# A new order of work in the chunks of a Mamba block, with a list of its own for the first chunk and loads of C waited for by groups

## The reference

```python
xi, z = split(x @ W_in.T)                        # 512 channels each
u = silu(causal_conv4(xi) + conv_b)
dbl = u @ W_xproj.T                              # 16 for dt, 16 for B, 16 for C
dt = softplus(dbl[..., :16] @ W_dt.T + b_dt);  A = -exp(A_log)
h = h * exp(dt * A) + (dt * u) * B;   y = sum_s h * C     # over 1024 tokens, 16 states
y = (y + u * D_skip) * silu(z)
x = layernorm(x + y @ W_out.T)
x = layernorm(x + (silu(x @ Wg.T) * (x @ Wu.T)) @ Wd.T)    # weights int / 127
```

## Time and profile before

| what | us |
|---|---|
| profiled execution | 1891.66 |
| its span | 1889.7 |
| first scan starts at | 34.3 |
| first chunk | 120.8 |
| steady chunks | 112.8 and 111.9 in turn |
| last chunk | 104.9 |
| from the last scan's end to the end of the span | 56.1 |
| busy: PE, DVE, ACT, POOL | 1763.2, 1708.9, 1656.7, 1498.0 |

### The profile page before, as it was taken

The page is one execution under the profiler, slowest core; times in us unless marked ns, Lnnn a source line. Parts: engine busy times, 40 slices in busy tenths (PEclk is TensorE's granted clock), DMA queues, the critical chain, the costliest instruction groups (busy, mean ns, idle before and its releaser), DMA issues.

```text
span 1889.7 us, 40293 instructions
## 1 busy us (share of the span) xinstructions
PE 1763.2 (93%) x15674; PEld 1218.9 (65%) x15674; DVE 1708.9 (90%) x1946; ACT 1656.7 (88%) x2892; POOL 1498.0 (79%) x847
## 2 busy tenths in 40 slices
...
GB/s 200 1 82 34 4 112 14 97 28 3 123 4 112 14 39 87 3 112 15 112 14 2 123 3 113 15 87 37 4 123 4 113 14 24 102 20 84 24 1 23
DMA packets 171341, 100.55 MB, mean 53 GB/s; under 512 B 139392, under 2 KB 157568, under 8 KB 162960
## 3 DMA queue, kind: packets, MB, share of 16 engines
...
## 4 chain that ended last, share of the span: by engine, by line
PE 48%; ACT 17%; DVE 17%; issue 11%; POOL 6%; DMA 0%; ACTq 0%; DVEq 0%; POOLq 0%
PE ring L1096 19%; PE tp L1075 14%; DVE h L846 8%; PE yb L1089 7%; ACT decay L641 6%; DVE acc L867 5%; ACT hT L648 5%; PE ring L1184 4%; POOL drive L512 3%; ACT acc L657 2%; ACT xi L659 1%; POOL diag_c L521 1%; ACT yt L669 1%; PE decay L1293 1%; ACT dt L695 1%
## 5 line engine op out<-in xcount | busy, mean ns | idle before, releaser
L512 POOL TENSOR_TENSOR drive<-dtu,b_all 128x1024 f32<-128x1024 f32 x512 | 1223.9, 2422 | 91.6 <-DVE h L846 78.8
L641 ACT ACTIVATE decay<-dt,a_neg 128x512 f32<-128x512 f32 x1024 | 707.8, 712 | 81.7 <-DVE h L846 80.6
L648 ACT ACTIVATE hT<-tp 128x512 f32<-128x512 f32 x1024 | 594.4, 611 | 81.9 <-PE tp L1075 80.8
L1075 PE MATMUL tp<-ident,h 128*128 128x128 f32 x4096 | 584.7, 280 | 80.5 <-ACT hT L648 71.0
L846 DVE TENSOR_TENSOR_SCAN h<-decay,h,drive 128x512 f32<-128x512 f32 x512 | 624.6, 1269 | 37.6 <-ACT decay L641 37.6
L846 DVE TENSOR_TENSOR_SCAN h<-decay,drive 128x512 f32<-128x512 f32 x512 | 597.2, 1211 | 61.4 <-ACT decay L641 44.1
L1075 PEld LDWEIGHTS tp<-ident,h 128*128 128x128 f32 x4096 | 465.5, 142 | 288.2 <-issue 140.3
L1089 PE MATMUL yb<-hT,diag_c 128*32 128x128 f32 x8192 | 275.5, 277 | 4.3 <-POOL diag_c L521 2.5
L1089 PEld LDWEIGHTS yb<-hT,diag_c 128*32 128x32 f32 x8192 | 210.7, 110 | 89.0 <-issue 53.2
L1096 PE MATMUL ring<-xt,w_in 128*128 128x512 f32 x512 | 241.9, 606 | 21.7 <-DVE yg L857 16.8
L867 DVE SCALAR_TENSOR_TENSOR acc<-xi,cw,acc 128x512 f32<-128x512 f32 x192 | 169.7, 898 | 14.8 <-ACT xi L659 10.8
(11 more groups left out here) (127 smaller groups left out, 1598.3 us busy)
## 6 DMA issues: line engine op xcount, KB each, us to landing
...
c_col<-bc_scratch SPq DMA_DIRECT2D x256, 2.0 KB, 2.4
...
```

Of the source, the lines that this page charges most:

```text
L512: tt(drive[:, j % 4, :, :], src, b_all[:, n:n + 2, :], ALU.mult).then_inc(g_dr, 1)
L641: act(decay[decay_slot(k.parity, i)][:, :], dt[:, cb, :], ACT.Exp, scale=a_neg[:, cb, n:n + 1]).then_inc(a_da, 1)
L648: act(hT[:, (64 * k.index + g) % HTS, :], tp[g % 2][:, :], ACT.Copy).then_inc(a_ev, 1)
L1075: last = nc.tensor.transpose(tp[g % 2][:, b * P:(b + 1) * P], h[:, h_slot(k.parity, q), t0:t0 + TS, :].rearrange("p t s -> p (t s)"), iden ...
```

## The change

The four steady tables are permuted. The first chunk gets tables of its own (`PE_FIRST`, `ACT_FIRST`, `DVE_FIRST`, `POOL_FIRST`), chosen by `table_of`. The tables of the last chunk and the lists of the end are reordered; `end_out 0 1` moves from the end list into the last chunk, `sz 3` and POOL's `gate 2` from the last chunk into the end lists. The loads of c_col count on four semaphores, one for each group of four states, and a diagonal waits for its group alone; in the first chunk each group's load of B goes directly before its four column loads.

```diff
 PE_SIDE = {
-    (0, 1): [("xi", 0), ("xi", 1), ("sum", 14)], (0, 3): [("xi", 2)], (1, 0): [("sum", 15), ("xi", 3), ("z", 0)],
-    (4, 3): [("out", 0)], (5, 0): [("out", 1)], (5, 2): [("sum", 3), ("xproj", 0)],
-    (6, 0): [("dt", 0), ("turn", 0)], (7, 0): [("x1T", 0), ("sum", 5)],
-    (14, 1): [("down", 0)], (14, 3): [("down", 1)],
+    (0, 1): [("xi", 0), ("xi", 1)], (0, 3): [("z", 0), ("sum", 14)], (3, 3): [("xi", 2), ("xi", 3)],
+    (4, 1): [("out", 0)], (4, 2): [("sum", 2), ("out", 1)], (4, 3): [("xproj", 0)],
+    (5, 2): [("sum", 3), ("dt", 0)], (5, 3): [("x1T", 0)], (6, 0): [("dt", 1), ("turn", 0)],
+    (14, 2): [("down", 0)], (15, 0): [("down", 1)],
...
 ACT_SIDE = {
-    (0, 0): [("log", 1)], (0, 1): [("hT", 60)], (0, 2): [("hT", 61), ("xi", 0)],
-    (0, 3): [("hT", 62), ("hT", 63)], (1, 0): [("xi", 1), ("xi", 2)], (1, 1): [("y", 3)], (1, 2): [("xi", 3)],
-    (5, 1): [("hT", 14), ("sz", 0), ("hT", 15), ("u", 0), ("u", 1), ("sz", 1), ("u", 2), ("sz", 2), ("hT", 16), ("sz", 3), ("u", 3)],
+    (0, 0): [("log", 1), ("hT", 60)], (0, 2): [("xi", 0), ("hT", 61), ("hT", 62), ("xi", 1), ("hT", 63)],
+    (3, 3): [("norm", 1), ("z", 3), ("hT", 10), ("hT", 11)], (4, 0): [("xi", 2), ("xi", 3)],
+    (4, 2): [("hT", 12), ("u", 0), ("sz", 0), ("sz", 1), ("u", 1), ("u", 2), ("sz", 2), ("u", 3), ("hT", 13)],
+    (5, 0): [("hT", 14), ("hT", 15), ("xproj", 0), ("hT", 16), ("hT", 17)],
+    (5, 1): [("norm", 0), ("hT", 18), ("bias", 0), ("y", 0), ("x1T", 0), ("hT", 19)], (5, 2): [("bias", 1)],
+    (8, 3): [("sz", 3)],
...
 DVE_SIDE = {
-    (0, 3): [("max", 1)], (2, 2): [("conv", 0, 0), ("conv", 0, 1)],
-    (5, 0): [("conv", 1, 0), ... , ("conv", 3, 0), ("r1", 0), ("conv", 3, 1)], (5, 2): [("r1", 1)],
-    (6, 1): [("skip", 0)], (13, 3): [("clamp", 0)], (15, 0): [("max", 0)],
+    (0, 3): [("conv", 0, 0)],
+    (4, 1): [("max", 1), ("conv", 0, 1), ("conv", 1, 0), ... , ("conv", 3, 0), ("conv", 3, 1)],
+    (4, 2): [("r1", 0)], (4, 3): [("r1", 1)], (5, 3): [("skip", 0)],
+    (13, 3): [("hid", 5), ("skip", 1)], (14, 0): [("clamp", 0), ("skip", 2)], (14, 3): [("max", 0)],
...
 POOL_SIDE = {
-    (5, 1): [("gate", 3), ("heads", 0), ("diag", 3)], (6, 1): [("std", 0)], (7, 0): [("gate", 0), ("dtu", 1)],
+    (4, 0): [("diag", 2), ("gate", 3)], (4, 1): [("heads", 0), ("diag", 3)], (5, 1): [("std", 0)],
+    (6, 1): [("dtu", 1)], (7, 1): [("gate", 0)],
...
+PE_FIRST = {
+    (0, 3): [("xi", 0), ("z", 0), ("xi", 1), ("z", 1), ("xi", 2), ("xi", 3), ("z", 2)], (1, 3): [("z", 3)],
...
+ACT_FIRST = {
+    (0, -1): [("xi", 0), ("z", 0), ("log", 1), ("z", 1), ("sz", 0), ("xi", 1), ("sz", 1), ("xi", 2), ("u", 0), ("z", 2)],
+    (0, 0): [("u", 1)], (1, 0): [("xi", 3), ("hT", 0)],
+    (7, 3): [("sz", 2), ("u", 2), ("hT", 28), ("sz", 3), ("u", 3)],
...
+DVE_FIRST = {
+    (0, -1): [("clamp", 1), ("conv", 0, 0), ("conv", 0, 1), ("conv", 1, 0), ("max", 1), ("conv", 1, 1), ("conv", 2, 0), ("conv", 2, 1)],
+    (7, 3): [("conv", 3, 0), ("conv", 3, 1), ("skip", 0)], (13, 2): [("skip", 1), ("clamp", 0)],
+    (14, 0): [("skip", 2)], (14, 1): [("max", 0)],
+POOL_FIRST = {
+    (0, -1): [("dtu", 1)], (2, 1): [("first_diag", 0)], (3, 0): [("first_diag", 1), ("first_diag", 2)],
+    (5, 0): [("first_diag", 3)], (8, 1): [("heads", 0)], (15, 0): [("gate", 0)],
+    (15, 1): [("gate", 1), ("dtu", 0), ("gate", 2), ("diag", 0)],
 PE_LAST = {
-    (14, 1): [("down", 0)], (14, 2): [("down", 1)], (15, 2): [("end_out", 0, 0)],
+    (12, 3): [("down", 0)], (13, 2): [("down", 1)], (14, 2): [("end_out", 0, 0)], (15, 1): [("end_out", 0, 1)],
 ACT_LAST = {
-    (5, 2): [("norm", 1), ("sz", 0), ("hT", 17), ("sz", 1), ("sz", 2), ("z", 3), ("hT", 18), ("sz", 3)],
+    (2, 2): [("sz", 0)], (12, 1): [("sz", 1), ("sz", 2)],
 ACT_END = [
-    ("hT", 57), ("hT", 58), ("hT", 59), ("end_hT", 60), ...
+    ("hT", 57), ("hT", 58), ("hT", 59), ("sz", 3), ("end_hT", 60), ...
 POOL_END = [
-    ("end_std", 1),
+    ("gate", 2), ("end_std", 1),

+def table_of(kind, steady, first, last):
+    return first if kind == "first" else last if kind == "last" else steady

-            def spread_bc(k, b_first=False):
+            def spread_bc(k, with_b=False):
                 wait(eng, a_dbl, k.count(2, 2))
                 eng.dma_start(bc_dram, dbl[R:R + 2 * N, :]).then_inc(st_bc, 16)
                 wait(eng, st_bc, k.count(16, 16))
-                if b_first:
-                    for g in range(4):
+                for g in range(4):
+                    if with_b:
                         load_b(g)
-                for n in range(N):
-                    g, s = n // 4, n % 4
-                    eng.dma_start(c_col[s:P - 3 + s:4, g, :], ...).then_inc(l_c, 16)
+                    for s in range(4):
+                        eng.dma_start(c_col[s:P - 3 + s:4, g, :], ...).then_inc(l_c[g], 16)
             def diagonals(k, g):
-                if g == 0:
-                    wait(eng, l_c, k.count(16 * N, 16 * N))
+                wait(eng, l_c[g], k.count(64, 64))
```

More of the change, by code:

```diff
@@ L62 @@
-    (15, 3): [("sum", 13)],
+    (0, 1): [("xi", 0), ("xi", 1)], (0, 3): [("z", 0), ("sum", 14)], (1, 0): [("sum", 15)], (1, 2): [("z", 1)],
+    (2, 0): [("z", 2), ("sum", 0)], (2, 1): [("turn", 3)], (3, 1): [("z", 3)], (3, 2): [("sum", 1)],
+    (3, 3): [("xi", 2), ("xi", 3)], (4, 1): [("out", 0)], (4, 2): [("sum", 2), ("out", 1)],
+    (4, 3): [("xproj", 0)], (5, 2): [("sum", 3), ("dt", 0)], (5, 3): [("x1T", 0)],
+    (6, 0): [("dt", 1), ("turn", 0)], (6, 1): [("sum", 4), ("x1T", 1), ("dt", 2), ("gate", 0)],
@@ L63 @@
+    (15, 0): [("down", 1)], (15, 3): [("sum", 13)],
 }
 ACT_SIDE = {
[18 rows of a table removed]
[18 rows of a table added]
 }
 DVE_SIDE = {
-    (0, -1): [("clamp", 1)], (0, 3): [("max", 1)], (2, 2): [("conv", 0, 0), ("conv", 0, 1)],
-    (3, 1): [("skip", 3)],
-    (5, 0): [("conv", 1, 0), ("conv", 1, 1), ("conv", 2, 0), ("conv", 2, 1), ("conv", 3, 0), ("r1", 0), ("conv", 3, 1)],
-    (5, 2): [("r1", 1)], (6, 1): [("skip", 0)], (7, 3): [("gs", 0)], (8, 1): [("hid", 0), ("gs", 1)],
-    (9, 0): [("hid", 1)], (9, 3): [("gs", 2)], (10, 0): [("hid", 2)], (10, 2): [("skip", 1)],
@@ L106 @@
-    (10, 3): [("gate", 3)], (11, 1): [("up", 3), ("gate", 4)], (11, 2): [("sum", 9)], (12, 0): [("gate", 5)],
-    (12, 2): [("sum", 10)], (12, 3): [("up", 4)], (13, 1): [("sum", 11)], (13, 2): [("up", 5)],
-    (14, 0): [("turn", 2)], (14, 1): [("down", 0)], (14, 2): [("down", 1)], (15, 0): [("sum", 12), ("sum", 13)],
-    (15, 2): [("end_out", 0, 0)],
+    (0, -1): [("z", 0)], (0, 0): [("sum", 14)], (1, 0): [("z", 1), ("sum", 15)], (2, 0): [("turn", 3)],
+    (2, 1): [("sum", 0)], (2, 2): [("out", 0)], (2, 3): [("out", 1)], (3, 1): [("z", 2)],
```

116 lines of the change are left out of this document (61 added, 55 removed), and 79 rows, old and new, of tables (ACT_FIRST, ACT_LAST, ACT_SIDE, DVE_LAST).

## The result

The kernel after takes 1844.06 us, the median of four runs (1842.64 to 1845.36), against 1891.05 us for the kernel before on the same chip: ratio 0.9757, 95% interval 0.9746 to 0.9769. The profiled execution took 1845.17 us, its span is 1843.2. Forecast was 1872 with a range of 1833 to 1901: the sign and the range held, the size did not. 47 us went, not 19.

What follows compares the result with a forecast made beforehand. No engine alone was taken to set the time but the order in which they meet, DVE being the steadiest pacer. Steady chunks -9, first -6, last -3, end -2 sum to -20 from 1891.66: 1872 us, range 1833 to 1901.

Steps and rivals of the forecast that it cites:

- The steady sum: Steady chunk: DVE loses 3.4 + 3.1 + 0.1 + 0.6 = 7.2 us against 7.8, 14 x -0.6 = -9 us.
- its list by place: DVE's losses per steady chunk before: 4.2 us in the opening, 3.0 behind the burst, 0.6 at chunk end: 7.8.
- Opening: Quads 0 to 2 of a steady chunk: DVE 3.4 us behind its bare work, against 4.2; bounds 2.0 and 5.8.
- The lone step: First convolution step in the steady opening: waits for xi 0 and, beside POOL's drives, up to one drive of 2.4 us.
- Burst and skip 0: Behind the steady convolution burst: skip 0 waits 2.6 us for its ring bank, with hand-overs 3.1, against 3.0.
- POOL idle at `heads` hides the burst: Steady chunk: `max` and eleven convolution steps, some 9.4 us, run while POOL waits at `heads`; its late drive 10 is covered.
- Lone silu: Slot (8,3), steady chunks: `sz 3` alone between decays adds two table loads, 2.6 us of ACT; DVE loses 0.1, bounds 0 and 2.6.
- Chunk end: Steady chunk's end: the 0.6 us loss for downs goes, the clamp beside POOL's last drives costs 0.6; bounds 0 and 4.5.
- First chunk, last chunk, end: Outside the steady chunks: -6 us (115 us long), -3 (bounds -7 and +4) and -2 (bounds -3 and +1).
- the five steps: First chunk: five convolution steps before scan 0 beside POOL's drives, 0.8 + 4 x 2.6 us, scan 0 at 56.5.
- The port case: Rival: clamp and first convolution lose 2 us a steady chunk to POOL's drives, 28 - 20 = +8, 1900 us; 7%.
- the case that the orders meet better: Rival: DVE loses 3.7 us a steady chunk less, 14 x -3.7 = -52, with the rest 1829 us; 20%.

Runs made afterwards that it cites:

- four orders made to shorten it: Kernel after with skip 0 two scans later, xi 1 later, norm 1 later, or work behind the burst spread: 1867.85, 1844.47, 1866.69, 1863.57 us.
- the three probes: Kernel after plus one unused DVE instruction per steady chunk: two-input beside drives 1881.62 us, one-input there 1884.43, two-input in the convolution burst 1843.29.
- max1_at_1_1: Kernel after with `max 1` alone moved from the head of the burst to behind scan (1,1), beside POOL's drives: 1869.40 us (0.9889 to the kernel before).
- conv01_at_2_2: Kernel after with three convolution steps of the steady burst moved back to slot (2,2), beside POOL's drives: 1941.21 us (1.0265 to the kernel before).
- its one attempt: Kernel before with three convolution steps of the steady chunks moved from slot (2,2) to the head of the burst at (5,0): 1920.60 us (1.0159).
- probe_one_at_8_1: Kernel after plus one unused DVE tensor_scalar with one SBUF input per steady chunk, behind scan (8,1) beside drives: 1884.43 us (0.9973 to the kernel before).

## Why the prediction was wrong in size

1. **The steady sum is the step that failed.** It forecast -0.6 us a chunk, 7.2 lost for 7.8, and -2.36 was measured. Measured in the same way, DVE's waits and what stands inside its instructions beside POOL, the chunk before lost 8.6: 6.0 of waits, and 10.62 - 12 x 0.75 = 1.6 in convolutions and 1.0 in `max`. The prediction's own first paragraph had these three numbers, 6.0 + 1.0 + 1.7 = 8.7, and its list by place came only to 7.8; 0.9 was dropped between two sentences. The chunk after loses about 6.5, not 7.2. So both terms were mis-sized, the loss before by 0.9 and the loss after by 0.7.
2. **Opening: forecast 3.4, measured 2.1** (waits of 0.42, 0.57, 0.23, 0.65 and 0.32 inside the convolution step in one chunk, 2.0 in the other). Two things were too large in it. Decay 5 was put at 9.4 us into the chunk, and scan 5, which waits for it, starts at 8.9. (The spacings it was added from, 0.5 for a copy and 0.6 for a decay, don't stand in the earlier trace rows; ACT's timeline of the kernel after has 0.48 and 0.61, so they were right.) The lone step was to lose up to a drive; it lost 0.32, because it comes so shortly before the end of one, and POOL's next drive was the longer one (2.81 for 2.38). That it meets the drive there was not foreseen; the lower bound of 2.0 (no drive met) covers the result. Of the 1.8 us a chunk between forecast and result, 0.9 are point 1 and 1.3 this one; points 3, 5 and 6 take 0.6 back, and 0.2 has no owner.
3. **Burst and skip 0: forecast 3.1, measured 3.50 and 2.83**, mean 3.2. Place, cause and length were right. What the forecast did not see is that this wait is not easily won back: four orders made to shorten it left the time or lengthened it.
4. **POOL idle at `heads` hides the burst: right.** All eleven steps 0.75 us, and 0.25 us more of DVE there cost nothing.
5. **Lone silu: forecast 0.1, measured 0.6 and 0.3 in one chunk and 0.2 in the next** at the decays behind it, 0.5 in the mean. It did not turn the result. The Trainium skill (ScalarE: Activation LUTs, section What ACT_TABLE_LOAD costs) adds 1380 ns of drain to each load; no run here shows it, the rows give 1.3 us per switch on either side of the silu.
6. **Chunk end: forecast no change, measured 0.7.** The clamp takes 0.70 in the mean of five, `max 0` waits 0.74 for ln in one chunk of two.
7. **First chunk, last chunk, end: -6, -3, -2 forecast, -6.8, -4.9, -1.7 measured.** Scan 0 was put at 56.5 and came at 57.6, the next chunk at 149 and came at 148.3; the five steps were put at 0.8 and four times 2.6, 11.2 us, and took 11.7, five times 2.35. The port was sized right here, from the earlier trace rows. In the last chunk DVE's waits were put at 7 for some 10 and are 5.4 for 9.7.
8. **The port case was set up on the wrong side.** The rivals asked whether DVE would lose more to POOL's drives after the change, at 7%. It loses 2.1 us a chunk less, and that is nearly the gain. That the time lies inside the stated range is owed to the case that the orders meet better (1829, 20%), and in part to luck: its reason was a more even PE, and the waits of DVE for `down` fell by no more than 0.5 us a chunk (1.8 to 0.7 in two chunks).

What is shown and what is argued: that an instruction with its operands in SBUF waits for the end of the running drive or of the next, and that the chunk pays most of that wait (more than all of it where the clock then falls), is shown by the three probes and `max1_at_1_1`. That the -2.36 is this price is bookkeeping (2.07 of it in the busy time of three lines), supported by `max1_at_1_1`, where one `max` beside drives gives back 1.90, and by the length of the steps in `conv01_at_2_2`. The kernel before with nothing but that price removed was not found: its one attempt got slower by its new waits. The rest, 0.3 us a chunk, is open.

The Trainium skill (SBUF — State Buffer, section Who interferes with whom) has a second clause that I had not used: besides instructions with two SBUF inputs, a tensor_scalar in a two-port mode takes the shared ports as well, and whoever comes first keeps them for its whole instruction. `probe_one_at_8_1` agrees (3.28 us in the mean; alone it was not timed, but the instruction of the same size with two inputs takes 0.25), and so does the batch-norm statistic, which has one SBUF input and is no such form: two of them take 0.75 us at 1244.19 in the kernel after, in the midst of POOL's drives from 1242.83 to 1247.52.
